# Batch 0's attention input moved in among batch 1's expert tiles, and batch 1's normalisation moved between the two sides of batch 0's one-hot table

## The reference, cut to what matters

```python
h = _layernorm(x) * (1 + ca) + sa
x = x + ga * _L0_attn_ref(h, ...)      # layer 0: a state-space scan over 32 heads
h = _layernorm(x) * (1 + cb) + sb
x = x + gb * _L0_ffn_ref(h, ...)       # layer 0: 8 experts of 128, top 2, and a shared one
h = _layernorm(x) * (1 + ca) + sa      # from here on layer 1's own modulation
x = x + ga * _L1_attn_ref(h, ...)
h = _layernorm(x) * (1 + cb) + sb
x = x + gb * _L1_ffn_ref(h, ...)

def _L1_attn_ref(x, Wq, Wk, Wv, Wo):   # 128 heads, head width 2, TOP_K = 32
    q = einsum('bsd,hd->bhs', x, Wq)
    keys = einsum('bsd,hd->bhs', x, Wk)
    v = x @ Wv.T                       # two values per head and token
    # per head: the 32 largest and the 32 smallest keys of the 512 tokens, with their values
    attn_top = softmax(q[..., None] * top_keys)
    attn_bot = softmax(q[..., None] * bot_keys)
    out = where(q > 0, attn_top @ top_vals, attn_bot @ bot_vals)
    return out @ Wo.T
```

## Time and profile before

| | us |
|---|---|
| median of 3 runs | 954.73 |
| lowest, highest | 953.02, 955.35 |
| the profiled execution, its own time | 956.11 |
| its span, first to last instruction | 954.3 |
| busy in the span: PE, DVE, ACT, POOL | 838.4, 791.0, 555.4, 463.9 |

### The profile page before, as it was taken

The page is one execution under the profiler, slowest core; times in us unless marked ns, Lnnn a source line. Parts: engine busy times, 40 slices in busy tenths (PEclk is TensorE's granted clock), DMA queues, the critical chain, the costliest instruction groups (busy, mean ns, idle before and its releaser), DMA issues. The chain is left out here.

```text
span 954.3 us, 16734 instructions
## 1 busy us (share of the span) xinstructions
PE 838.4 (88%) x5486; PEld 590.4 (62%) x5486; DVE 791.0 (83%) x1749; ACT 555.4 (58%) x1225; POOL 463.9 (49%) x459
## 2 busy tenths in 40 slices
PE   4778999999999999999999889989985785688897
PEld 3556677777677767777777667746553633345555
DVE  6978999999999999999888989786679878856752
ACT  3657877777778777777867667312123382552321
POOL 2146677676776655545544434545223122424652
PEclk9979999999999999999999999999997787899999
DMA  7013443343433432222333122422204113402122
GB/s 265 29 30 109 139 132 115 114 132 117 138 113 105 137 106 68 77 81 96 103 89 89 50 84 67 150 78 79 89 34 102 31 17 52 144 0 67 56 91 78
DMA packets 52662, 87.16 MB, mean 91 GB/s; under 512 B 5824, under 2 KB 23744, under 8 KB 51808
## 3 DMA queue, kind: packets, MB, share of 16 engines
q1 hardware_dynamic: 43360, 73.50, 26.0%
q10 hardware_dynamic: 9216, 12.59, 3.6%
HBM read 70.67 MB, written 15.40 MB: 90 GB/s over the span
## 5 line engine op out<-in xcount | busy, mean ns | idle before, releaser
L616 PE MATMUL bank<-hTs,wA 128*128 128x512 bf16 x768 | 180.1, 382 | 0.5 <-DVE u L1866 0.5
L2445 POOL TENSOR_TENSOR xbuf<-xbuf,dec 128x384 f32<-128x384 f32 x64 | 53.4, 834 | 211.7 <-ACT xbuf L1338 169.6
L1866 DVE SCALAR_TENSOR_TENSOR u<-bank,chn,u 128x511 f32<-128x511 f32 (+2 forms) x192 | 142.8, 744 | 3.5
L616 PEld LDWEIGHTS bank<-hTs,wA 128*128 128x128 bf16 x768 | 75.5, 99 | 83.4 <-issue 5.0
L688 PE MATMUL bank<-wB,yb 128*128 128x256 f32 x512 | 121.1, 380 | 0.7 <-DVE acc L1822 0.7
L688 PEld LDWEIGHTS bank<-wB,yb 128*128 128x128 f32 x512 | 92.5, 190 | 11.2 <-issue 1.1
L2455 POOL TENSOR_TENSOR yb<-yv,gs 128x512 f32<-128x512 f32 x64 | 81.8, 1277 | 14.1 <-DVE yv L1893 13.9
L767 PE MATMUL bank<-Mm,xbuf 128*128 128x128 f32 x512 | 71.8, 284 | 18.7 <-DVE yv L1893 17.5
L767 PEld LDWEIGHTS bank<-Mm,xbuf 128*128 128x128 f32 x512 | 65.9, 196 | 30.1 <-issue 21.2
L1348 ACT ACTIVATE rel<-csb,cs 128x128 f32<-128x128 f32 x256 | 82.4, 416 | 0.0
L1338 ACT ACTIVATE xbuf<-bank,dtv 128x128 f32<-128x128 f32 x256 | 72.8, 372 | 14.1 <-PE bank L733 14.1
(11 more groups left out here) (277 smaller groups left out, 1854.1 us busy)
## 6 DMA issues: line engine op xcount, KB each, us to landing
csb<-csd SPq DMA_DIRECT2D x64, 256.0 KB, 3.5
wA<-in_win SPq DMA_DIRECT2D x32, 256.0 KB, 4.4
wAd<-wA ACTq DMA_DIRECT2D x32, 256.0 KB, 4.4
wA<-wAd SPq DMA_DIRECT2D x32, 256.0 KB, 3.7
wB<-in_wob SPq DMA_DIRECT2D x8, 512.0 KB, 6.0
wBd<-wB ACTq DMA_DIRECT2D x32, 128.0 KB, 4.3
wB<-wBd SPq DMA_DIRECT2D x8, 512.0 KB, 5.5
sS<-cbd SPq DMA_DIRECT2D x16, 256.0 KB, 3.4
```

The source lines that it names most:

```text
L616: last = nc.tensor.matmul(out, wpart(a, kt), hpart(c, kt), start=n == 0, stop=n == 5)
L1866: nc.vector.scalar_tensor_tensor(out=u[:, n % 2, d:S], in0=bank[0][:, 0:S - d], scalar=chn[:, hid, 3 - d:4 - d], in1=u[:, n % 2, d:S], op0 ...
```

## The change

It moves six things.

- **Memory.** `OH` is allocated before `wqkv`, so that it and no longer `wqkv` lies over the expert weights; `KT_` shares a new buffer `ktv` with batch 0's copied keys and values.
- **SP.** `wqk`, `wv` and `wo` are loaded before `weight_rows(0, 1)` and no longer wait for the last expert product; the gather of batch 0's query words no longer waits for `xf_done`.
- **Batch 0's input among the tiles.** DVE: `add_experts(0)` at m = 9 instead of 10, statistics and root at 10, normalised rows at 11, clears at 12 and 13, `extremes` at 14, one `next_eight` and `strike_eight` in each of 14 to 17; `first_batch` now stands after `hidden`. TensorE: rows turned at m = 12 before `rows_out`, and after `rows_out` keys and queries at 12, values at 13, turned keys at 15. ACT: modulation at 12, `keys_queries` and the copies for the choice (formerly DVE's) at 13, values kept at 14, shifted keys at 15, turned keys kept at 17. POOL: the three steps of batch 0's query words at 13, 14 and 15, half of the first piece of `PV` at 16 and half at 17.
- **Words of batch 0** are now cut on POOL as batch 1's are (16 instructions, of which 12 come after the last tile); `first_words` and `less_piece` are gone.
- **Batch 1's normalisation.** Statistics, root and rows of batch 1 stood at the start of `heads()` and behind `extremes(0)`; now they stand after `one_hots(0, 0)` and before `one_hots(0, 1)`.
- **TensorE's list in `heads()`** is now: codes 0, rows 1, keys and queries 1, gate rows, values 1, turned queries, table side 0, table side 1.

```diff
@@ sync @@
-            weight_rows(0, 1)
-            sp.wait_ge(q["fu"], B * FT[0])
             sp.dma_start(wqk[:], io["wqk"]).then_inc(q["d_attn"], 16)
             sp.dma_start(wv[:], io["wv"]).then_inc(q["d_attn"], 16)
             sp.dma_start(wo[:], io["wo"]).then_inc(q["d_attn"], 16)
+            weight_rows(0, 1)
...
-                    sp.wait_ge(q["xf_done"], B)
@@ tensor, experts(0) @@
+                    if m == 12:
+                        for ft in range(KT):
+                            turned_rows(2, 0, ft, bank[6 + ft])
+
+                def heads_begun(m):
+
+                    if m == 12:
+                        pe.wait_ge(q["d_attn"], 48)
+                        keys_queries(0)
+                    if m == 13:
+                        pe.wait_ge(q["a_qkc"], 1)
+                        pe.wait_ge(q["a_qr"], 1)
+                        for half in range(2):
+                            last = values(0, half, bank[6 + half])
+                        last.then_inc(q["a_v"], 1)
+                    if m == 15:
+                        pe.wait_ge(q["a_pvs"], 2)
+                        for n in range(2):
+                            turned_keys(0, n, bank[6 + n]).then_inc(q["a_kT"], 1)
...
                     rows_out(m)
+                    if L == 0:
+                        heads_begun(m)
@@ tensor, heads() @@
-                for ft in range(KT):
-                    turned_rows(2, 0, ft, bank[ft])
-                pe.wait_ge(q["d_attn"], 48)
-                keys_queries(0)
-                pe.wait_ge(q["xf_done"], B)
-                for half in range(2):
-                    last = values(0, half, bank[5 + half])
-                last.then_inc(q["a_v"], 1)
+                turned_codes(0)
+                pe.wait_ge(q["a_pvs"], 4)
                 for ft in range(KT):
                     turned_rows(2, 1, ft, bank[(2, 7)[ft]])
-                for m in range(2):
-                    turned_keys(0, m, bank[3 + m]).then_inc(q["a_kT"], 1)
                 keys_queries(1)
                 pe.wait_ge(q["d_wm"], 32 + 16 * KT)
                 pe.wait_ge(q["scb_done"], 2)
                 pe.wait_ge(q["a_qkc"], 2)
                 for n in range(2):
                     gate_rows(lambda kt: wm1[kt], scb1, 3 * n + 2, bank[(2, 1)[n]])
-                less_piece(0, "a_p0")
                 pe.wait_ge(q["gm_done"], 4)
-                turned_codes(0)
-                less_piece(1, "a_p2")
-                pe.wait_ge(q["a_cTc"], 1)
                 for half in range(2):
                     last = values(1, half, bank[1 + half])
@@ scalar, experts(0) @@
+                    if L == 0 and m == 12:
+                        act.wait_ge(q["modb_done"], 2)
+                        for ft in range(KT):
+                            modulated(2, 1, 0, ft, bank[6 + ft])
+                    if L == 0 and m == 13:
+                        keys_queries(0)
+                        choice_starts(0)
+                    if L == 0 and m == 14:
+                        values_kept(0, (ktv[:, 2 * S:3 * S], ktv[:, 3 * S:]), bank[6:8])
+                    if L == 0 and m == 15:
+                        shifted_keys(0)
+                    if L == 0 and m == 17:
+                        for n in range(2):
+                            act.wait_ge(q["a_kT"], n + 1)
+                            nc.scalar.activation(ktv[:, n * S:(n + 1) * S], bank[6 + n][:, :], ACT.Copy)\
+                                .then_inc(q["a_pvs"], 1)
@@ vector, experts(0) @@
+                    if m == 10:
+                        row_stats(0, 1)
+                        row_roots(0, 1)
+                    if m == 11:
+                        normal_rows(0, 1)
+                    if m == 12:
+                        nc.vector.memset(KW[:], 0.0)
+                        link(nc.vector.tensor_scalar(minus4[:], block4, -1.0, None, ALU.mult))
+                    if m == 13:
+                        link(nc.vector.tensor_copy(VW[:, :, :, 4], block4.unsqueeze(1).to_broadcast([P, NQ, QG])))
+                    if m == 14:
+                        extremes(0)
+                    if m > 13:
+                        next_eight(0, m - 14, m % 2)
+                        strike_eight(0, m - 14, m % 2)
...
-                    if L == 0:
-                        first_batch(m)
                     hidden(m)
...
-                    if m == last_tile(L, 0) + 2:
+                    if m == last_tile(L, 0) + 1 + L:
                         add_experts(0)
+                    if L == 0:
+                        first_batch(m)
                 add_experts(1)
@@ vector, heads() @@
-                row_stats(1, B)
...
-                choice_starts()
-                extremes(0)
-                row_roots(1, B)
-                normal_rows(1, B, xh1)
-                for r in range(K // 8):
-                    next_eight(0, r, r % 2)
-                    strike_eight(0, r, r % 2)
                 for part in range(3):
                     choice_ends(0, part)
...
                 codes_taken(0)
                 one_hots(0, 0, 0, K)
+                row_stats(1, B)
+                row_roots(1, B)
+                normal_rows(1, B, xh1)
                 for b in range(B):
 
                     one_hots(b, 1, 0, K)
@@ gpsimd @@
+                    if L == 0 and 13 <= m < 16:
+                        query_words(0, m - 13)
+                    if L == 0 and m > 15:
+                        for step in range(2):
+                            pieces(0, 0, 2 * (m - 16) + step)
...
+                for n in range(1, 4):
+                    for step in range(4):
+                        pieces(0, n, step)
+                for step in range(3):
+                    query_words(1, step)
                 pool.wait_ge(q["a_vw"], NQ // 4)
-                for n, qq in enumerate((2, 3, 0, 1)):
-                    rounded(0, "a_pvs", n, qq).then_inc(q["a_p0"], 1)
-                    piece(0, "a_p0", None, n, qq).then_inc(q["a_p1"], 1)
-                    rounded(1, "a_p1", n, qq).then_inc(q["a_p2"], 1)
-                    piece(1, "a_p2", PV[:, :, 2, qq, :], n, qq).then_inc(q["a_pv"], 1)
+                for n in range(4):
+                    for step in range(4):
+                        pieces(1, n, step)
```

More of the change, by code:

```diff
@@ L839, in _, with keys_queries, values, turned_keys @@
             drain()
+            def keys_queries(b):
+                pe.wait_ge(q["hT_done"], 8 + KT * (b + 1))
+                hb = slice(b * S, (b + 1) * S)
+                for m in (1, 0):
+                    for kt in range(KT):
+                        last = nc.tensor.matmul(bank[(QA, KA)[m][b]][:, :], wqk[:, m, kt, :], hT[:, kt, hb],
+                                                start=kt == 0, stop=kt == KT - 1)
+                    last.then_inc(q["a_qk"], 1)
+            def values(b, half, out):
+                for t in range(2):
+                    tok = (b * TB + 2 * half + t) * P
+                    for kt in range(KT):
+                        last = nc.tensor.matmul(out[:, t * D:(t + 1) * D], hT[:, kt, tok:tok + P], wv[:, kt, :],
+                                                start=kt == 0 and t == 0, stop=kt == KT - 1,
+                                                skip_group_check=True)
+                return last
+            def turned_keys(b, m, out):
+                pe.wait_ge(q["a_kd"], 2 * b + m + 1)
+                for t in range(TB):
+                    last = nc.tensor.matmul(out[:, t * P:(t + 1) * P], kd[:, m, t * P:(t + 1) * P], ident,
+                                            is_transpose=True, start=t == 0, stop=True, skip_group_check=True)
+                return last
             def experts(L):
@@ L1530, in heads @@
-                keys_queries(0)
-                def shifted_keys(b):
-                    for side in range(2):
-                        act.wait_ge(q["a_ext"], 2 * b + side + 1)
-                        if b:
-                            act.wait_ge(q["a_kT"], 2)
-                        nc.scalar.activation(kd[:, side, :], ks[:, b, :], ACT.Identity,
-                                             bias=ext[:, b, side:side + 1]).then_inc(q["a_kd"], 1)
-                def kept_values(row, qq, half, turned):
-                    return nc.scalar.activation(
-                        row[:, half * 2 * P:(half + 1) * 2 * P].rearrange("p (t h) -> p t h", t=2),
-                        turned[:, :].rearrange("p (t j h) -> p t j h", t=2, j=2)[:, :, qq - 2, :], ACT.Copy)
@@ L1558, in heads @@
                     gate_copied(2 + n, bank[(2, 1)[n]])
-                first_words(1, "a_p2")
-                first_words(2, "a_pv")
-                act.wait_ge(q["a_v"], 2)
-                for qq in (2, 3):
-                    for half in range(2):
-                        last = kept_values(v1[:, qq - 2, :], qq, half, bank[1 + half])
-                    last.then_inc(q["a_pvs"], 1)
+                values_kept(1, (v1[:, 0, :], v1[:, 1, :]), bank[1:3])
```

(19 more changed lines are left out.)

289 lines of the change are left out of this document (115 added, 174 removed).

## The result

The changed kernel takes **966.29 us** (median of 4 runs, 962.67 to 970.61) beside 955.04 us for the kernel before on the same chip (4 runs, 953.02 to 961.62). The ratio is 1.0109, interval 1.0066 to 1.0151: slower, by 10.4 us as the ratio has it (the two medians lie 11.2 us apart). The profiled execution took 970.61 us, span 968.8, so the profile shows 14.5 us more than that of before (954.3).

A forecast was written before the change was run, and what follows sets the result against it. TensorE bounds the expert tiles, DVE the stretch behind. Tiles +9.9, DVE to 744.2 and a 19.0 us chain put side 1 at 763.2, +8.2; less 1.0, net +7.2: 961.9 us, range 953.5 to 968.2.

The forecast's parts named there:

- The tiles: Expert tiles on TensorE: 9.3 us of added work and 0.6 more waiting, last output 9.9 us later, at 716.4.
- TensorE waits 1.3 us: Tile m = 10: batch 0's statistics and root cost DVE 4.2 us, making TensorE wait 1.3 us.
- DVE up to ready rows: DVE from last output to batch 1's rows: adding, choice's end, side 0 one-hots, normalisation, POOL's hold-up; 716.4 to 744.2 us.
- I take half, 6.2 us: DVE behind the tiles: POOL's remaining pieces, 12.3 us, hold DVE up for half their time, 6.2 us.
- A: Rival: POOL and DVE take strict turns, all 12.3 us count, +6.2 more, 968.1 us; chance 0.12.
- B: Rival: POOL costs DVE nothing behind the tiles, net +1.0, 955.7 us, no change; chance 0.13.
- The page's stricter rule: DVE and POOL's shared ports as exclusive lock: ready lists alternate, nearly all 12.3 us on DVE, 6 more than taken.
- The chain: TensorE from batch 1's normalised rows to table side 1: 11.3 + values 3.62 + turned queries 0.7 + side 0 3.37, 19.0 us.
- the 11.3 us hold a slow start already: TensorE's chain up to the second gate: 11.3 us from the earlier kernel already includes a low clock after a pause.
- Side 1: Table side 1 on TensorE runs without a gap behind side 0, 3.37 in place of 4.38 us: -1.0.
- Rival C: Moved TensorE work falls into the tiles' waits, 5.9 us vanish and B holds: -4.9, 949.8 us; chance 0.13.
- I am wrong if the first one-hot is written before 729: Failure signs: first one-hot before 729, last output before 713, or something other than batch 1's rows ending TensorE's wait.

The follow-up runs named there:

- e9: Kernel before with only batch 1's normalisation moved between the two sides of the one-hots, nothing moved into the tiles: 964.46 us, ratio 1.0079.
- e2: Changed kernel with batch 1's normalisation put back ahead of batch 0's choice ends, moves into the tiles kept: 953.54 us, ratio 0.9964.
- e1: Changed kernel run again without an edit, 6 runs: 966.88 us, ratio 1.0096 to the kernel before.
- e4: Changed kernel with fourteen unread matmuls on TensorE behind side 0's one-hots, ahead of batch 1's rows: 961.61 us, ratio 1.0055.
- e6: Changed kernel with the edits of e3 and e4 together: 958.09 us, ratio 1.0025.
- e3: Changed kernel with POOL's pieces 1 to 3 of batch 0 waiting until batch 1's rows are written: 960.93 us, ratio 1.0045.
- e8: e2 with codes turned between batch 1's keys and queries, and batch 0's root split over tiles 10 and 11: 950.85 us, ratio 0.9949.

## Why the prediction was right, and where its terms were off

Slower, in the range, and for the reason forecast: batch 1's normalisation starts a chain on TensorE that ends last. e9 shows it by doing that part alone, e2 by undoing it. Term by term:

- **The tiles, forecast +9.9.** Last output at 722.56 against 706.5 is 16.0, less the 3.2 that were there at the first output: +12.8 us (e1 +11.6, e2 to e4 +9.4 to +9.8). So the size is right where the clock holds, but partly by luck, since the waits in it miss to both sides. "TensorE waits 1.3 us" for the statistics and root at m = 10: it waits before tile 11's output, 2.02 us here and 1.85 to 2.03 in e1 to e6. "Some 0.4 us for the modulated rows" at m = 12: no wait is left there. The last two waits are 1.44 and 1.94 us (I gave 2.0 and 2.2). Over that come, in this profile, 1.37 us for the late weights of tile 10, and in it and e1 1.6 us for the output of tile 11 and the products of tile 14 at a lower clock (products 3.79 and 4.38 us in place of 2.75). The forecast had no term for that. The windows of the changed kernel over TensorE (length, busy, PEclk, DMA share, GB/s) have the clock at full until the waiting output and lower from there on, while in e3 the granted clock stays at 1.00 ahead of its wait of 2.03 us and behind it:

```profile
685.00:688.40 3.40, 1.40 (x7) 1.00 0.13 49
688.40:691.00 2.60, 2.58 (x14) 0.63 0.12 43
691.00:695.00 4.00, 4.00 (x21) 0.81 0.19 66
```

- **DVE up to ready rows.** 722.56 to 749.0 is 26.4 us; forecast 716.4 to 744.2, 27.8. The unblocked choice is 5.9 us (e3), not 6.9: two hits take 0.76 us together, where I had counted twice 0.83. "I take half, 6.2 us" for POOL was measured by e3 as 5.8: rivals A (12.3) and B (nothing) both fall. That it came out so near is luck, as half was a choice between two bounds. And the upper bound was too high: two of the fourteen pieces start before the last output ends (720.84 and 721.53 us), so that twelve, 10.6 us by the earlier trace rows, run beside DVE's list.
- **The page's stricter rule.** The Trainium skill (SBUF — State Buffer, "SBUF: two separate sides") gives the pair of ports, of two instructions that need it, to whichever starts first, for the whole instruction, and the other is blocked. The traces agree that each side blocks the other: in e3 POOL's copy loses 6.3 us to DVE's list, in the changed kernel DVE loses 5.8 us. What I had made of it, two ready lists that take turns with nearly all on DVE's account, did not come: the bill is split, and in e2 and e3 a POOL instruction that starts behind the first one-hot stands out not one instruction but the whole list.
- **The chain, forecast 19.0.** It took 770.25 - 749.0 = 21.2 us. The step "the 11.3 us hold a slow start already" failed: keys and queries took 6.36 us, where the kernel before has 4.09 for the same eight (from 724.91), and e4 3.70. Windows over TensorE alone (length, busy, PEclk, DMA share, GB/s) show it at the lower level, half clock (1.2 GHz), until behind 757:

```profile
748.00:751.00 3.00, 1.85 (x8) 0.50 0.03 8
751.00:754.00 3.00, 2.13 (x4) 0.50 0.00 0
754.00:757.00 3.00, 3.00 (x5) 0.50 0.00 0
757.00:760.00 3.00, 3.00 (x12) 0.94 0.00 0
```

  Before it TensorE had done 2.02 us of work in 28. In e4 the fourteen matmuls run just before, and the same windows' view gives a full clock from the keys on (the rows ahead of them take 1.09 us in place of 1.94):

```profile
746.00:749.00 3.00, 2.44 (x6) 1.00 0.00 0
```

  The Trainium skill (TensorE: Matmul & The Clock Gate, "Part 1: The HAM clock gate") has the clock halve after idling; the trace agrees. I had named that price, then left it out because the kernel before starts that chain "after a pause as well"; but the earlier trace rows gave it 18.02 us of TensorE work in those 28 us at a mean clock of 0.70, and the new one 2.02.
- **Side 1, forecast -1.0:** 0.9 us come back.
- **Sum.** The kernel measured by the stretch: +12.1 against +8.2. The excess is tiles 2.9, chain 2.2, less 1.4 on DVE: 3.7 of 3.9 us. Against the medians the miss is smaller: 10.4 or 11.2 us (ratio, medians), in e1 9.2 or 10.2, in place of 7.2.
- **Rival C** wanted the moved work to fall into the tiles' waits: the waits before outputs came to 6.8 us in all (5.6 in e1). A faster kernel is in this change, but e2 finds it in the order of DVE's list and not in the tiles' waits.
- **"I am wrong if the first one-hot is written before 729"** and the other two tests: 735.58 us, last output 722.56, rows ended TensorE's wait. All held.

Left open: why the slowed products appear in both profiles of the changed kernel and not in those of e2 to e6, whose tiles are the same code and which wait as long before tile 11's output (1.85 to 2.03 us against 2.02 and 2.03); how often executions without a profile have them; and what makes the 3.2 us ahead of the first output.

## What to carry to other kernels

Moving work off the busy engine into an earlier stage can take away the cover of what stays: in the list of the busy engine, place the step that starts the other engine's longest chain first (here ahead of the choice's end, -1.3% of the kernel), and behind it what that chain needs only in its later half. When a wait becomes long, add to its price the lower clock of what follows (here 3.4 us for a wait of 14), and look at which helper engine works beside the list that is now on the path.

## What the runs showed of the hardware that was not expected

- **DVE and POOL don't split their hold-up evenly.** A POOL instruction that started 0.16 us into a list of 32 back-to-back one-hots (6.58 us, not lengthened at all) lasted 6.89 us in place of 0.61 (e3), and one that started 1.5 us into a list of 64 lasted 13.57 us in place of 2.13 (e2): each stood out the whole list, not one instruction. But where POOL's pieces were already running when the one-hots began (changed kernel, side 0), DVE lost 1.3 us (7.91 against 6.58), and against the choice's end, from the first hit to the first one-hot, it lost 4.1 us (10.0 against 5.9). What decides between the two wasn't tried.
- **After the same short wait the clock fell in some executions and not in others.** Behind a wait of 2.02 us twelve products took 3.79 us, behind one of 2.03 us eleven took 4.38 (e1); behind waits of 1.85 to 2.03 us in e2 to e6 they took 2.75.
- **Matmuls that nobody reads shortened the chain behind them:** 4.4 us of them, inside a wait, took 3.4 us off it (e4).
- **The same code drifts by 5 us between executions:** the first expert tile's output, with the same code ahead of it in e1 to e8, starts between 627.4 and 632.6 us. A difference of two profiles below that size has to be taken from a common point on.
